# Dealing the copies of turned rows to two engines in another order, in the second cross-attention of a two-layer decoder

## What is computed

```
scores = jnp.einsum('bhmd,bhnd->bhmn', q, k)
scores = jnp.where(mask, scores, jnp.float32(-10000000000.0))
attn = jax.nn.softmax(scores / jnp.sqrt(jnp.float32(DK)), axis=3)
out = jnp.einsum('bhmn,bhnv->bhmv', attn, v)
out = out.transpose(0, 2, 1, 3).reshape(bs, n_q, EDIM)
return out @ Wo.T + bo
```

## Time and profile before

| what | value |
|---|---|
| median of three runs | 827.79 us |
| time of the profiled execution | 827.26 us |
| span of the profiled execution | 825.5 us |
| TensorE matmuls busy | 779.8 us, 94% of the span |
| VectorE busy | 649.5 us, 79% |
| ScalarE busy | 615.8 us, 75% |
| GpSimd busy | 427.8 us, 52% |

### The profile page before, as it was taken

One profiled execution on the slowest core, in us unless ns is written; L12 is line 12 of the kernel. 1 busy time (PEld: TensorE's weight loads), 2 busy tenths in 40 slices (PEclk: granted clock), 3 DMA queues, 4 the chain that ended last, 5 costly groups with the idle time before them and its releaser, 6 DMA issues.

```text
span 825.5 us, 20952 instructions
## 1 busy us (share of the span) xinstructions
PE 779.8 (94%) x6901; PEld 596.4 (72%) x6901; DVE 649.5 (79%) x2458; ACT 615.8 (75%) x1602; POOL 427.8 (52%) x461
## 2 busy tenths in 40 slices
PE   9998899999988988999999999999999999999996
PEld 7876677777666766677777777777676777677786
DVE  3997778888998867688777767775888888986777
ACT  4547898888884367888888887885999999984331
POOL 0265465667845145553555544225865666335764
PEclk9999999999999999999999999999999999999999
DMA  9401661222101458988989889865122222100001
GB/s 314 151 26 39 199 204 37 85 84 85 72 15 71 185 177 246 302 244 267 272 239 283 257 250 280 267 184 179 43 69 69 68 69 69 66 1 1 23 30 52
DMA packets 105393, 115.05 MB, mean 139 GB/s; under 512 B 29061, under 2 KB 94085, under 8 KB 105030
## 3 DMA queue, kind: packets, MB, share of 16 engines
q1 hardware_dynamic: 104724, 113.35, 43.5%
q10 hardware_dynamic: 562, 0.35, 0.1%
HBM read 48.09 MB, written 51.82 MB: 121 GB/s over the span
## 4 chain that ended last, share of the span: by engine, by line
PE 49%; ACT 7%; DVE 5%; issue 2%; DMA 1%; POOL 1%; SPq 0%; DVEq 0%; ACTq 0%
PE bank L1563 7%; PE bank L242 6%; PE bank L2327 6%; PE bank L250 5%; PE bank L2344 3%; PE bank L2313 3%; PE bank L1578 3%; PE bank L1614 3%; PE bank L1604 3%; PE bank L1547 2%; PE bank L2379 2%; ACT Sx L1770 2%; PE bank L2361 1%; PE bank L234 1%; ACT q_heads L1778 1%
## 5 line engine op out<-in xcount | busy, mean ns | idle before, releaser
L242 PE MATMUL bank<-x_feat,w_all_mats 128*128 128x256 f32 x384 | 93.4, 388 | 1.9 <-ACT q_full L358 0.6
L242 PEld LDWEIGHTS bank<-x_feat,w_all_mats 128*128 128x128 f32 x384 | 70.7, 192 | 14.8 <-ACT rw L2702 3.8
L2660 ACT ACTIVATE bias_area<-bias_area,mq_two 128x256 f32<-128x256 f32 x128 | 66.6, 536 | 0.0
L3056 POOL TENSOR_TENSOR bnd<-bnd,consts 128x60 f32<-128x60 f32 x64 | 18.5, 311 | 81.1 <-DMA bnd<-band_scratch 81.0
L3045 POOL COPY rw<-rw 128x856 f32<-128x856 f32 x32 | 29.0, 905 | 57.9 <-ACT rw L2702 57.9
L894 ACT ACTIVATE dist<-dist,mq_two 128x256 f32<-128x256 f32 x128 | 56.1, 503 | 3.5 <-DVE mq_two L1005 3.5
L2836 DVE COPY q_heads<-bank 128x512 f32<-128x512 f32 x64 | 41.7, 685 | 21.1 <-PE bank L2327 21.1
L1770 ACT ACTIVATE Sx<-Sx,mq 128x256 f32<-128x256 f32 x128 | 54.3, 501 | 2.3 <-DVE mq L1868 2.3
L1876 DVE COPY q_heads<-bank 128x512 f32<-128x512 f32 x64 | 42.1, 685 | 17.0 <-PE bank L1563 17.0
L1005 DVE CUSTOM_DVE_ANT_0 dist<-bank,bias_area 128x256 f32<-128x256 f32 x128 | 46.5, 420 | 10.7 <-PE bank L701 5.6
L1770 ACT ACTIVATE Pr<-Pr,mq 128x256 f32<-128x256 f32 x128 | 54.5, 505 | 0.0
(11 more groups left out here) (322 smaller groups left out, 2377.9 us busy)
## 6 DMA issues: line engine op xcount, KB each, us to landing
dist<-skew_scratch SPq DMA_DIRECT2D x64, 296.0 KB, 4.2
skew_scratch<-rw SPq DMA_DIRECT2D x30, 588.0 KB, 5.2
bnd<-band_scratch SPq DMA_DIRECT2D x64, 108.0 KB, 2.7
band_scratch<-bias_area SPq DMA_DIRECT2D x32, 162.0 KB, 3.3
band_scratch<-bias_area SPq DMA_DIRECT2D x32, 148.0 KB, 2.6
skew_scratch<-dist SPq DMA_DIRECT2D x4, 1024.0 KB, 8.4
context_values<-dist SPq DMA_DIRECT2D x8, 512.0 KB, 2.6
v_two<-context_values SPq DMA_DIRECT2D x8, 512.0 KB, 4.2
```

Source lines behind the costliest of these rows:

```text
L242: last = pe.matmul(dst[:, m * S:(m + 1) * S], w[:, k, m * P:(m + 1) * P], rhs[:, k, :], start=(k == 0), stop=(k == FT - 1))
L2660: last = act.activation(rows_of(n, g)[:, t, :], rows_of(n, g)[:, t, :], ACT.Exp, bias=mq_two[:, n % 2, g, t:t + 1], scale=-1.0, accum_out= ...
```

## The change

VectorE now copies the turned rows of g = 0 and 2, ScalarE those of g = 1 and 3. So each of the two banks has one engine that reads it. On VectorE the copy of g = 2 of round n - 1 stands between the scans of `peaks(n, 1)` and those of `peaks(n, 2)`; the copy of g = 0 stays behind the scans. On ScalarE the copy of g = 1 of round n - 1 takes the place that the copy of g = 2 had, ahead of `exps(n, 0)`. The waits of `turn` follow: turns 0 and 2 wait for VectorE's copies, turns 1 and 3 for ScalarE's. One copy after the last round is added on VectorE for g = 2 of round 31. Three lines fewer stand in `turn`, so what was L1563 is L1560 in the new kernel, L1868 is L1865, and so on.

```
 def turn(n, g):

     pe.wait_ge(p_exp, 4 * n + g + 1)
-    if g < 2:
-        ge(pe, pt_act, 2 * (n - 1) + g + 1)
-    else:
-        pe.wait_ge(pt_dve, 2 * n + g - 1)
+    ge(pe, (pt_dve, pt_act)[g % 2], 2 * n + g // 2)
...
 # mask_act
         if n >= 1:
-            turned(n - 1, 2)
+            turned(n - 1, 1)
         exps(n, 0)
         exps(n, 1)
...
-turned(NQ * B - 1, 2)
+turned(NQ * B - 1, 1)
 turned(NQ * B - 1, 3)
...
 # mask_dve
         peaks(n, 0)
         peaks(n, 1)
+        if n >= 1:
+            turned(n - 1, 2)
         if j == 2 and b >= 1:
             normalise(b - 1, 0)
         peaks(n, 2)
...
-        turned(n, 1)
+
+turned(NQ * B - 1, 2)
```

## The result

The changed kernel takes 839.22 us in the median of four runs (837.31 to 840.51); the kernel before, run beside it, 827.56 us. The ratio is 1.0141, with a 95% interval from 1.0113 to 1.0170: slower by 1.4%. The forecast was 838.1 us in a range of 832 to 842, so the time lies inside it. The profiled execution of the changed kernel took 840.08 us.

What follows compares the result with a forecast made beforehand. TensorE's order was taken as the bound, in a ring with nearly full ScalarE and VectorE. Three places, 1.90 us a batch, gave 9.5 us over five batches plus 1.3 at the ends: 827.26 + 10.8 = 838.1 us, range 832 to 842.

Steps and rivals of the forecast that it cites:

- What bounds the kernel: TensorE, busy 94% of the span: time can be won or lost only where its order is held up.
- Copies 0 and 3 cost nothing: Copy 0 stays behind VectorE's scans and copy 3 between ScalarE's exponentials: nothing added.
- Place A: Third round: turn 3 waits for copy 1, now late on ScalarE; 0.79 us a batch (0.73 to 0.85).
- Place B: Fourth round: turn 3 waits for copy 1, behind ScalarE's copy of the output sum; 0.60 us a batch.
- Place C: VectorE's unbroken stretch to the third round's second normalisation holds three copies instead of two; 0.51 us a batch.
- They add: The three places lie one behind the other on the same ring of engines: 1.90 us a batch (1.84 to 2.05).
- How often: The full sequence of the three places occurs five times, from batches 1 to 6: 9.5 us (9.2 to 10.3).
- the ends: Partial sequences in the first and last batches: 1.3 us taken, between -0.15 and 2.7.
- The copies alternate better: Rival, faster: one reader per bank, ScalarE no longer waits for turn 2; up to 5.7 us, 821.6 us, chance 0.06.
- Its other form: Same faster rival, room judged by weight loads' 71% share: 11.6 us over eight batches, 815.7 us; shared chance 0.06.
- No change: Rival: turn 3's delay falls into time in which VectorE and ScalarE wait anyway; 827.3 us, chance 0.07.
- One or two places are covered: Rival, slower by less: ScalarE ends its round earlier, so Place A or Place B shrinks; 831.1 to 835.1 us, chance 0.13.

## Why the prediction was right

*What bounds the kernel.* TensorE's order, and what holds it up. The page after has the same busy times in a longer span, and the time lies in 12.9 us of idle TensorE ahead of turns 2 and 3. Right.

*Copies 0 and 3 cost nothing.* Right for the time. Copy 0 of the second round came later, though, and turn 2 waits 0.45 us for it, which the forecast didn't have. In the change this costs nothing: VectorE doesn't pause from 667.25 to 676.30, and A, B and C make up the period without it. It shows only where copy 2 is taken away.

*Place A, 0.79 us.* It measures 0.64, outside its bounds of 0.73 to 0.85. The term that was mis-sized is the small one, what comes back: I took 0.14 us from the end of VectorE's product to TensorE's turning of A, as between a copy and a turn. In the new kernel TensorE is hardly behind there, the product ends at 653.96 and L234 starts at 654.01, so the release takes 0.05 us. The scores ahead of L234 started 0.70 us before it, about as in the kernel before (0.68), so this one start could be TensorE's own pace; but in the kernel with the useless copy ahead, TensorE stands idle for 0.88 us before L234 and the 0.05 is the same (product's end 704.13, L234 704.18). In the kernel before L234 started 0.26 after the product's end (648.58 - 648.32), so 0.21 of the 0.85 comes back and not 0.12 or less: 0.64. Giving the third round's copy back changed the period by 0.64, the same figure.

*Place B, 0.60 us.* It measures 0.61, and 0.64 by the experiment, which also gives back the 0.03 behind it. Right.

*Place C, 0.51 us.* It measures 0.56. The scans won 0.08 us by standing behind one copy less, for 0.09 forecast, and the stretch behind them grew by 0.64 for one copy, where I took 0.60. A copy on VectorE still holds the next instruction for 0.60 us, 653.87 to 654.47 in the timeline, not for its 0.68. That the stretch is on the ring is shown by the useless copy ahead of the normalisation; the one behind changed nothing. But undoing the copy 2 of one round gave back 0.27 only, because the path over turn 3 of the second round then ends last. So the place is right in the change, with a second path close behind it.

*They add.* 0.64 + 0.61 + 0.56 = 1.81, against 1.85 of the period; the runs that undo A, B and both, and the one that is the sum of two others, agree to within 0.01. The forecast period of 23.2 is 23.13.

*How often.* The weighing of batch 1's third round stands at 609.38 before and 611.97 after; less the 2.01 of the later start of the stage that is 0.58 us of growth. From there to batch 6's it was 104.66 us (to 714.04) and is 113.90 (to 725.87): 9.24 us in five steps, for 9.5 forecast. The last 1.01 lies behind. So the ends hold 1.59 us, for 1.3 taken (the upper bound of 2.7 was added up from the middle terms; with the places' own bounds it is 2.9). At the start, the 0.88 us at 584.66 that might vanish shrank to 0.31:

```profile
586.23 0.63 PE L1560 MATMUL bank<-ident,Sx 128*128 128x128 f32 x4 [0.31 <-ACT q_heads L1775]
```

The sum was 10.8 for 10.83 measured. That it is so close is luck: the five steps were too large by 0.26, most of it from A, and the ends too small by 0.29. The medians lie 11.66 us apart (839.22 - 827.56), 0.83 more than the stage grew, and the profiled executions 12.82; their 2.0 us lie ahead of the stage, in code that is the same.

*The rivals.* "The copies alternate better" had its fact right: ScalarE's idle time ahead of its copies fell by 5.1 us. It came back elsewhere: ScalarE's idle time ahead of the exponentials that read `Sx` rose from 2.3 to 7.0 us, and ahead of its copy of q from 1.3 to 6.9. Its other form, which took room from the share of weight loads, fell as well: they are busy 15.17 us of a batch of 23.13, as they were 15.16 of 21.30, and the batch got longer. The Trainium skill (Perfetto Trace Analysis, Identifying the Most-Contended Engine) would read that as more room; here the orders tried brought the period down to 20.90 us at best. "No change" rested on waits of ScalarE and VectorE; A and B hit TensorE, as the new waits show. "One or two places are covered" fell because each of the three grew by 0.56 us or more.

## What to carry to other kernels

Where several engines form a ring and each is nearly full, the order of equal work is worth more than its amount: find for each moved instruction who waits for its end and what stands ahead of it on its new engine, from start times in one timeline, and add the places up only if they lie one behind the other. One instruction type needs pricing by place, since copy 1, given back, gained 0.64 us in each of two rounds and lost 0.62 in the two others together, and a useless copy cost 0.94 at one point of VectorE's list and nothing 1.3 us further on (where it was also shorter). And a place that is taken away gives back only what the next path leaves: 0.27 of 0.56 for C. To shorten such a ring, look first at what the bounding engine already waits for in the kernel as it is; here one copy made one exponential group earlier gave 0.25%.

## What the runs showed of the hardware

*A copy from SBUF to SBUF on VectorE took 0.42 us, or 1.02 where GpSimd was already at work.* The useless copy ahead of the normalisation, over its seven executions (shortest, median, longest, ns), and the one behind:

```profile
L1921 DVE COPY xn<-w_all_mats x7: 419/1021/1032, 606.8 to 750.4; 128x512 f32<-128x512 f32 x7
```

```profile
L1930 DVE COPY xn<-w_all_mats x7: 414/415/416, 605.7 to 742.7; 128x512 f32<-128x512 f32 x7
```

GpSimd's timeline in the first of the two kernels, where VectorE's copy ran from 654.28 to 655.31:

```profile
653.60 1.43 POOL L2071 TENSOR_TENSOR x_tok<-x_tok,bias_rep 128x256 f32<-128x256 f32 x2
654.96 0.82 POOL L2102 CAST glu_x_even<-x_feat 128x512 fp32r<-128x512 f32 x1
```

All six long copies of the first kernel began while GpSimd ran L2071, and GpSimd was idle at the short one (606.76; its last work had ended at 605.24). In the second kernel three copies fell where GpSimd was idle, and four (652.04, 675.17, 698.29, 721.42) began within 0.02 us of the end of its cast. Those four stayed at 0.42 us, and it was GpSimd's next instruction, begun during the copy, that was longer: 1.45 to 1.47 us, for 1.28 in the changed kernel. The first kernel's cast beside the long copy took 0.82 us, for 0.61 in the second. The Trainium skill (SBUF — State Buffer, SBUF: two separate sides) says that VectorE in its faster modes and GpSimd share a pair of ports under an exclusive lock, and that the one that starts first keeps them for its whole instruction while the other blocks. The trace agrees with that order, with 1.02 against 0.42 us where GpSimd was first and about 0.18 us more on GpSimd where VectorE was; no run here separates the lock from another cause. The kernel's own copies, which read PSUM, keep 0.68 to 0.69 us on average in the kernels looked at. So the useless copy wasn't the fixed size that I meant it to be, and its price is read from its rows.

*The granted clock fell twice in one execution, inside a busy stage.* In the kernel with the useless copy ahead, the windows around 705 us and one at 754 (columns as above) read:

```profile
701.00:705.00 4.00, 3.04 (x37) 2.40 (x34) 3.97 (x17) 2.13 (x7) 3.92 (x5) 1.00 0.10 26
705.00:709.00 4.00, 3.39 (x14) 2.74 (x14) 3.08 (x17) 2.54 (x6) 0.26 (x1) 0.69 0.00 0
709.00:713.00 4.00, 4.00 (x44) 2.29 (x44) 0.69 (x1) 2.82 (x8) 1.84 (x2) 0.88 0.01 4
...
754.00:758.00 4.00, 3.89 (x23) 2.15 (x24) 2.08 (x11) 3.90 (x10) 0.00 (x0) 0.57 0.00 0
```

and TensorE's timeline at the first of the two:

```profile
704.18 0.65 PE L234 MATMUL bank<-ident,at 128*128 128x128 f32 x4 [0.88 <-DVE at L1889]
...
706.10 0.68 PE L1560 MATMUL bank<-ident,Pr 128*128 128x128 f32 x4 [0.61 <-ACT q_heads L1775]
706.57 3.57 PE L242 MATMUL bank<-x_feat,w_all_mats 128*128 128x256 f32 x8
```

The q projection took 3.57 us instead of 1.89, about twice as long, as at the 1.2 GHz level; ahead of it TensorE had stood still for 0.88 and 0.61 us within 3 us. That batch took 25.74 us where the others took 24.06. The second fall came behind the same two waits (0.87 us at 752.19 and 0.61 at 754.11), and the weighing there took 1.94 us for 1.07. But the same pair of waits stands in four other batches of this execution, at 631.98, 656.06, 680.12 and 729.93, and there the clock stayed at 1.00: the 4 us from 676.94 have TensorE busy for 3.05 us, as the 3.04 from 701.00, and no fall behind them. So these waits alone don't make the clock fall, and what decides it stays open. In the stage of the kernel before and of the changed one the clock is 1.00 in every window of 4 us. It was one execution, and whether the drops return wasn't tried; here they cost about 3 us.
